# A two-layer graph kernel: five piece buffers in place of four, a shorter ring of rounded tiles, and the features loaded in six parts

## The chip, the cores and the metric

One core of one Trainium2 chip runs the kernel. The metric is the device time of one execution in microseconds. The engines are named as in the profile: PE (TensorE matmul), PEld (its weight loads), DVE (VectorE), ACT (ScalarE), POOL (GpSimd), SP (SyncE), and a trailing q (ACTq, SPq) is that engine's instruction queue, which issues DMAs.

## The reference

`x` is 4096 nodes by 128 features and `adj` a 4096 by 4096 float32 matrix (64 MiB) that is needed three times.

```python
h = relu(layernorm(x))
x = x + (adj.T @ h) / adj.sum(axis=0)[:, None]   # 0 where the sum is 0
h = relu(layernorm(x))
x1 = swish((adj @ h) @ W + b)
x2 = swish((adj @ x1) @ W + b)
return x + x2
```

## The kernel before

The kernel reads `adj` in three sweeps. No scheduler is involved: the program of each engine is written out by hand, and the order in the code is the order on the engine.

**Float32 products.** PE multiplies a float32 tile either whole (L367, L444) or split in two parts. For a split tile ACT writes the rounded part (`a_hi` at L542, `at_hi` in `hi3`, L584), POOL or DVE writes the rest (`a_lo` at L855, `at_lo` in `lo3`, L203), and PE then makes three cheap products: two with the rounded tile (main, L372 and L373, or L450 and L451) and one with the rest (L387, L461). A whole tile costs PE more time and the other engines nothing.

**Sweep 1** (`adj.T @ h`) takes 64 pairs of row tiles, v = 0 to 63, 16 to each quarter of the columns; a pair is 1 MiB and is loaded by SP (`load1`, L328) into one of `RAW1` = 5 buffers. `WHOLE1_FIRST`, `WHOLE1` and `WHOLE1_LAST` say which pairs of a quarter go whole. In the first quarter 6, 8, 9, 11, 12 and 14 are split. For each of them POOL first makes the rest of the features, `h_lo` (L846), and then the two rests of the pair, `a_lo` (L855). PE's main products of a split pair wait for `h_lo` (`h_lo_ready`, L360). Features of pairs that are split only later (`LATE_ROWS`) are rounded at the end of the quarter. DVE adds each pair to the degree sums (L699). The features `x_rows` themselves arrive in parts, `HEAD`, each loaded ahead of the pair in `HEAD_PAIRS`; for each part DVE makes statistics (L680, L683), POOL scale and shift (L833 to L838), and ACT the normed rows `h` (L509).

**Sweeps 2 and 3** (`adj @ h`, `adj @ x1`) are 8 groups of 512 nodes each, of four **pieces** of 2 MiB (512 rows by 1024 columns), in the order of `PIECES`. A piece is loaded in four blocks of 512 KB, 32 partitions each: SP issues blocks 0 and 1, ACT blocks 2 and 3 (`load3`, L285). There are `RAW3` = 4 piece buffers (`raw3`). A piece has four **units**; DVE turns a unit (`turn3`, L744) into one of `TURN` = 9 places of `turned`, or, for a few units, into PSUM (`dg`); its rest goes to the same place number of `at_lo`. ACT's rounded tiles lie in a ring of `RING3` = 6 places; ACT waits there until PE's main products and the rest of the unit six splits earlier are done (L581 to L583). PE makes main3 of a unit and then rest3 of the unit two before (`REST_LAG`). In a group of 16 units, 0, 5, 10 and 15 are whole; in even groups DVE makes the rests of units 3 and 13, in odd ones of 3, 8 and 13, and POOL all others.

After a pair of groups: ACT copies the sums out (`copy_n`, L592), PE multiplies by W (`xw`, L474), DVE adds the bias, ACT makes the swish (L600) and, in sweep 2, the rounded features of sweep 3 (L608), whose rest POOL makes (L869). Sweep 3 begins with the group that sweep 2 ended with, and the last four pieces of sweep 2 (`KEPT`) are used from their buffers and not loaded again.

**ACT's loop** (L638 to L659) does for each unit: `hi3(unit)`; in every fourth unit both blocks of the piece three ahead (L644, L645); then copies and swish when due. The two DMA issues stand in the same queue as the roundings, so a rounding behind them waits until they are issued.

```python
for unit in range(UNITS3):
    if not whole3(unit) and unit not in AHEAD3:
        hi3(unit)
    i = unit // QU + RAW3 - 1
    if unit == 1:
        load3(act, 3, ACT_BLOCKS)
    if unit % QU == 0 and RAW3 <= i < len(PIECES) and i not in KEPT:
        load3(act, i, ACT_BLOCKS)
```

Of the kernel before, what the change touches and what calls it, by code (L numbers as in the profile page):

```python
# [59 lines left out]
def build(nc, x_in, adj, w_in, b_in, out):  # L60
# [10 lines left out]
    with ctx:  # L71
# [40 lines left out]
        raw3 = {3: sb("raw3_3", [P, GB, BC], into=sweep2)}  # L112
        nT = sb("nT", [P, QC], into=sweep2)
        zs = sb("zs", [P, QT, P], into=sweep2)
        w = sb("w", [P, P], into=sweep2)
        bias = sb("bias", [P, P], into=sweep2)
        at_hi = sb("at_hi", [P, RING3, UC, GROUP], f32r, into=sweep2)
        for n in (1, 2):
            raw3[n] = sb(f"raw3_{n}", [P, GB, BC], into=sweep2)
        spare = sb("spare", [P, 256], into=sweep2)  # L120
# [79 lines left out]
        def lo3(eng, unit):  # L200
            s = split3(unit)
            eng.wait_ge(hi3_done, s + 1)
            return eng.tensor_tensor(at_lo[:, place(unit)], turned_tile(unit), at_hi[:, ring3(s)].bitcast(f32),  # L203
                                     ALU.subtract)
# [27 lines left out]
        def group_after(unit, later, hurried):  # L232

            ends = [n for n in range(2 * GROUPS) if last_unit(n) == unit - (hurried if n == GROUPS - 1 else later)]
            return ends[0] if ends else None
# [26 lines left out]
        def raw3_free(eng, i):  # L262
# [43 lines left out]

        def turned_nodes(dst, half=None):
# [10 lines left out]
        def _(sp):  # L318
# [30 lines left out]
        def _(pe):  # L349
# [76 lines left out]
            def main3(unit):  # L426
# [27 lines left out]
            def rest3(unit):  # L454
# [52 lines left out]
        def _(act):  # L507
# [63 lines left out]
            def hi3(unit):  # L571
# [12 lines left out]
                act.activation(at_hi[:, ring3(s)], turned_tile(unit), ACT.Copy).then_inc(hi3_done, 1)  # L584

            def copy_n(n):
                r = pair_of(n)
                act.wait_ge(main3_done, last_unit(n) + 1)
                act.wait_ge(rest3_done, split3(last_unit(n) - 1) + 1)
# [48 lines left out]
            for unit in range(UNITS3):  # L638
# [30 lines left out]
        def _(dve):  # L669
# [151 lines left out]
        def _(pool):  # L821
# [51 lines left out]
            for b, (lo, hi) in enumerate(HEAD):  # L873
                scale_shift(lo, hi, b)
            for v in splits1:
# [6 lines left out]
                lo1(v)  # L882
                if q >= 1 and k == 14:
# [38 lines left out]
```

## Time and profile before

| what | value |
|---|---|
| median of three runs (lowest, highest) | 626.46 us (625.41, 627.19) |
| the profiled execution's own time | 627.91 us |
| its span on the core | 626.1 us |
| PE busy | 609.1 us, 97% |
| POOL busy, DVE busy, ACT busy | 544.2, 541.8, 345.8 us |
| moved by DMA | 197.73 MB, mean 316 GB/s |
| granted TensorE clock | 0.998 of full speed |

Sweep 1 fills the span up to about 223 us, sweep 2 up to 423, sweep 3 the rest. A busy PE in this table is the union of overlapping records; where two records of PE follow each other without a gap it has no time to give.

### The profile page before, as it was taken

How to read it: one execution, taken by the hardware profiler on the slowest of the kernel's cores; microseconds unless marked ns; L12 is line 12 of the kernel's file. 1: busy time of each engine (PE TensorE's matmuls, PEld its weight loads, DVE VectorE, ACT ScalarE, POOL GpSimd, SP SyncE). 2: the span in 40 equal slices, each digit the busy share in tenths (PEclk: the TensorE clock that was granted, in tenths of full speed). 3: DMA queues.
4: the chain of work that ended last, by engine and by line, in shares of the span. 5: the costliest groups of instructions: out<-in, count | busy, mean ns of one | idle time of the engine just before them, and what ended most of it. 6: DMA issues, size and time to landing. Idle time of an engine off the chain costs nothing.

```text
span 626.1 us, 6939 instructions
## 1 busy us (share of the span) xinstructions
PE 609.1 (97%) x2296; PEld 413.3 (66%) x2296; DVE 541.8 (87%) x558; ACT 345.8 (55%) x456; POOL 544.2 (87%) x281
## 2 busy tenths in 40 slices
PE   8888999999999999999999999999999999999996
PEld 5355666577565567667667667777677677677774
DVE  5899699787868999897998998997998998998991
ACT  2493686595263354756656646646555546456551
POOL 2499799599688588999999989997999999998991
PEclk9999999999999999999999999999999999999999
DMA  9998999889999899999999999909999999999961
GB/s 324 382 372 301 339 320 358 293 329 275 353 351 367 287 345 334 347 347 347 347 347 348 347 348 347 283 25 220 308 348 349 348 349 348 348 348 349 348 176 34
DMA packets 151492, 197.73 MB, mean 316 GB/s; under 512 B 5280, under 2 KB 134560, under 8 KB 151456
## 3 DMA queue, kind: packets, MB, share of 16 engines
q1 hardware_dynamic: 86176, 132.92, 63.9%
q10 hardware_dynamic: 65280, 64.36, 33.6%
q8 instruction: 18, 0.29, 0.2%
q14 instruction: 18, 0.15, 0.1%
HBM read 195.17 MB, written 2.10 MB: 315 GB/s over the span
## 4 chain that ended last, share of the span: by engine, by line
PE 63%; POOL 10%; DMA 9%; issue 6%; DVE 6%; ACT 3%; ACTq 2%; SPq 1%; POOLq 0%; DVEq 0%
PE dg L444 14%; PE dg L461 11%; PE dg L451 11%; PE dg L450 11%; DMA raw<-in_adj_dram 9%; PE m_ps L367 7%; POOL a_lo L855 5%; POOL at_lo L203 3%; PE m_ps L372 2%; PE m_ps L387 2%; PE m_ps L373 2%; DVE dg L699 2%; PE m_ps L474 2%; ACTq L285 2%; DVE turned L744 2%
## 5 line engine op out<-in xcount | busy, mean ns | idle before, releaser
L203 POOL TENSOR_TENSOR at_lo<-turned,at_hi 128x1024 fp32r<-128x1024 f32 x152 | 358.9, 2402 | 26.5 <-ACT at_hi L584 26.4
L744 DVE STREAM_TRANSPOSE turned<-raw 128x1024 f32<-128x1024 f32 x216 | 257.7, 1221 | 20.2 <-PE dg L461 13.9
L584 ACT ACTIVATE at_hi<-turned 128x1024 fp32r<-128x1024 f32 x152 | 157.0, 1055 | 97.8 <-DVE turned L744 71.1
L855 POOL TENSOR_TENSOR a_lo<-raw,a_hi 128x1024 fp32r<-128x1024 f32 x62 | 145.9, 2391 | 21.7 <-ACT a_hi L542 21.6
L699 DVE TENSOR_TENSOR dg<-raw,dg 128x2048 f32<-128x2048 f32 x60 | 137.5, 2291 | 29.2 <-DMA raw<-in_adj_dram 27.6
L450 PE MATMUL dg<-at_hi,f_hi 128*128 128x512 f32 x384 | 152.4, 397 | 0.3 <-ACT at_hi L584 0.2
L451 PE MATMUL dg<-at_hi,f_lo 128*128 128x512 f32 x384 | 151.3, 394 | 0.0
L461 PE MATMUL dg<-at_lo,f_hi 128*128 128x512 f32 x384 | 145.1, 459 | 1.2 <-POOL at_lo L203 1.2
L444 PE MATMUL dg<-turned,f_w 128*128 128x512 f32 x256 | 120.2, 592 | 0.0
L367 PE MATMUL m_ps<-raw,h 128*128 128x512 f32 x264 | 117.8, 593 | 2.5 <-DMA raw<-in_adj_dram 1.7
L461 PEld LDWEIGHTS dg<-at_lo,f_hi 128*128 128x128 f32 x384 | 72.1, 188 | 43.3 <-issue 28.9
L367 PEld LDWEIGHTS m_ps<-raw,h 128*128 128x128 f32 x264 | 49.7, 189 | 55.5 <-issue 49.9
L542 ACT ACTIVATE a_hi<-raw 128x1024 fp32r<-128x1024 f32 x62 | 62.4, 1051 | 42.9 <-DMA raw<-in_adj_dram 41.9
L450 PEld LDWEIGHTS dg<-at_hi,f_hi 128*128 128x128 f32 x384 | 72.2, 188 | 17.9 <-ACT at_hi L584 1.4
L451 PEld LDWEIGHTS dg<-at_hi,f_lo 128*128 128x128 f32 x384 | 72.1, 188 | 16.8 <-issue 0.5
L444 PEld LDWEIGHTS dg<-turned,f_w 128*128 128x128 f32 x256 | 48.4, 189 | 36.5 <-issue 31.2
L372 PE MATMUL m_ps<-a_hi,h_hi 128*128 128x512 f32 x124 | 51.1, 412 | 5.4 <-issue 3.8
L203 DVE TENSOR_TENSOR at_lo<-dg,at_hi 128x1024 fp32r<-128x1024 f32 x40 | 47.6, 1189 | 3.9 <-ACT at_hi L584 3.9
L744 DVE STREAM_TRANSPOSE dg<-raw 128x1024 f32<-128x1024 f32 x40 | 49.3, 1233 | 1.7 <-PE dg L461 0.8
L373 PE MATMUL m_ps<-a_hi,h_lo 128*128 128x512 f32 x124 | 48.4, 391 | 0.0
L584 ACT ACTIVATE at_hi<-dg 128x1024 fp32r<-128x1024 f32 x40 | 40.8, 1020 | 13.3 <-DVE turned L744 9.3
L387 PE MATMUL m_ps<-a_lo,h_hi 128*128 128x512 f32 x124 | 42.4, 459 | 0.0
(55 smaller groups left out, 338.1 us busy)
## 6 DMA issues: line engine op xcount, KB each, us to landing
raw<-in_adj_dram SPq DMA_DIRECT2D x64, 1024.0 KB, 7.3
raw<-in_adj_dram ACTq DMA_DIRECT2D x122, 512.0 KB, 14.2
raw<-in_adj_dram SPq DMA_DIRECT2D x118, 512.0 KB, 12.5
out_dram<-x SPq DMA_DIRECT2D x12, 128.0 KB, 6.6
x_rows<-in_x_dram SPq DMA_DIRECT2D x2, 256.0 KB, 5.4
x_rows<-in_x_dram SPq DMA_DIRECT2D x1, 512.0 KB, 11.2
out_dram<-x SPq DMA_DIRECT2D x4, 64.0 KB, 1.8
out_dram<-x ACTq DMA_DIRECT2D x4, 64.0 KB, 2.0
```

The costliest lines, as they stand in the source:

```text
L203: return eng.tensor_tensor(at_lo[:, place(unit)], turned_tile(unit), at_hi[:, ring3(s)].bitcast(f32), ALU.subtract)
L367: mm = pe.matmul(acc, h[:, 2 * k + i], raw1[:, v % RAW1, i, cols], start=first, stop=last)
L372: pe.matmul(acc, h_hi[:, r], a_hi[:, s % RING1, cols], start=first, stop=False)
L444: mm = pe.matmul(acc, f_w[:, UC * WHOLE3.index(j) + c], turned[:, place(unit), c], start=first and c == 0, stop=False)
L450: pe.matmul(acc, f_hi[:, r + c], at_hi[:, s, c], start=first and c == 0, stop=False)
L451: mm = pe.matmul(acc, f_lo[:, r + c], at_hi[:, s, c], start=False, stop=False)
L461: mm = pe.matmul(dg[:, 0, (n % 2) * 512:(n % 2 + 1) * 512], f_hi[:, r + c], at_lo[:, place(unit), c], start=False, stop=unit + 1 == last_u ...
L542: act.activation(a_hi[:, s % RING1], raw1[:, v % RAW1, i], ACT.Copy).then_inc(hi1_done, 1)
L584: act.activation(at_hi[:, ring3(s)], turned_tile(unit), ACT.Copy).then_inc(hi3_done, 1)
L699: dve.tensor_tensor(dg[:, :, :], src, dg[:, :, :], ALU.add).then_inc(deg_added, 1)
L744: dve.transpose(dst, src).then_inc(t3_done, 1)
L855: pool.tensor_tensor(a_lo[:, s % RING1], raw1[:, v % RAW1, i], a_hi[:, s % RING1].bitcast(f32), ALU.subtract).then_inc(lo1_done, 1)
```

## The change

Six edits, made together.

1. The features come in six parts, ahead of pairs 0, 0, 1, 3, 5 and 7, where there were four, ahead of pairs 0, 2, 3 and 4. POOL's scale and shift of the sixth part stand behind its first split pair.
2. Pair 8 of the first quarter goes whole there, and is among the late rows.
3. A fifth piece buffer. It may be filled once sweep 1 is done on PE and DVE. Five pieces are kept between the sweeps.
4. The room comes from `turned` and `at_lo` (nine places become eight) and from the ring of rounded tiles (six become three).
5. ACT's two block issues of a piece stand two units apart.
6. The last two groups of sweep 2, and the first two of sweep 3, alternate piece by piece, so that each piece kept is again the one needed.

```diff
-HEAD = ((0, 4), (4, 8), (8, 16), (16, 32))
-HEAD_PAIRS = (0, 2, 3, 4)
+HEAD = ((0, 2), (2, 4), (4, 8), (8, 16), (16, 24), (24, 32))
+HEAD_PAIRS = (0, 0, 1, 3, 5, 7)
-WHOLE1_FIRST = (0, 1, 2, 3, 4, 5, 7, 10, 13, 15)
-LATE_ROWS = (2, 3, 5)
-SPLIT_ROWS = (6, 8, 9, 11, 12, 14) + LATE_ROWS
+WHOLE1_FIRST = (0, 1, 2, 3, 4, 5, 7, 8, 10, 13, 15)
+LATE_ROWS = (2, 3, 5, 8)
+SPLIT_ROWS = (6, 9, 11, 12, 14) + LATE_ROWS
-RAW3 = 4
-TURN = 9
-TURN_OFF = 4
+RAW3 = 5
+TURN = 8
+TURN_OFF = 3
-RING3 = 6
-RING_OFF = 2
+RING3 = 3
-PIECES = FIRST + tuple((n, q) for n in range(2, 2 * GROUPS) for q in range(QUARTERS))
+TAIL2 = ((6, 3), (7, 3), (6, 2), (7, 0), (6, 0), (7, 1), (6, 1), (7, 2))
+HEAD3 = tuple((n, q) for q in range(QUARTERS) for n in (GROUPS, GROUPS + 1))
+PIECES = (FIRST + tuple((n, q) for n in range(2, GROUPS - 2) for q in range(QUARTERS)) + TAIL2 + HEAD3
+          + tuple((n, q) for n in range(GROUPS + 2, 2 * GROUPS) for q in range(QUARTERS)))
...
         def raw3_free(eng, i):
...
+            elif i == 4:
+
+                eng.wait_ge(main1_done, QUARTERS * PAIRS)
+                eng.wait_ge(deg_added, QUARTERS * PAIRS)
...
             def hi3(unit):
...
-                if s == RING3 - RING_OFF:
-                    act.wait_ge(main1_done, QUARTERS * PAIRS)
-                    act.wait_ge(deg_added, QUARTERS * PAIRS)
                 if s >= RING3:
                     act.wait_ge(main3_done, splits3[s - RING3] + 1)
                     wait_lo3(act, splits3[s - RING3])
-                act.activation(at_hi[:, ring3(s)], turned_tile(unit), ACT.Copy).then_inc(hi3_done, 1)
+                act.activation(at_hi[:, s % RING3], turned_tile(unit), ACT.Copy).then_inc(hi3_done, 1)
...
-                if unit == 1:
-                    load3(act, 3, ACT_BLOCKS)
-                if unit % QU == 0 and RAW3 <= i < len(PIECES) and i not in KEPT:
-                    load3(act, i, ACT_BLOCKS)
+                if unit in (1, 2, 3, 5):
+                    load3(act, 3 + unit // 3, ACT_BLOCKS[(1, 2, 3, 5).index(unit) % 2:][:1])
+
+                if unit % QU in (0, 2) and RAW3 <= i < len(PIECES) and i not in KEPT:
+                    load3(act, i, ACT_BLOCKS[unit % QU // 2:unit % QU // 2 + 1])
...
-            for b, (lo, hi) in enumerate(HEAD):
+            for b, (lo, hi) in enumerate(HEAD[:-1]):
                 scale_shift(lo, hi, b)
...
                 lo1(v)
+                if v == splits1[0]:
+                    scale_shift(*HEAD[-1], len(HEAD) - 1)
```

**POOL in the first quarter.** `norm` are the columns of scale and shift, `h_lo` the rest of a pair's features, `a_lo` the rests of the pair. POOL before, from its fourth scale and shift on (line numbers of the kernel before):

```order
L833 TENSOR_TENSOR norm<-mv,consts 128x16
L834 TENSOR_TENSOR norm<-mv,consts 128x16
L836 TENSOR_TENSOR norm<-norm,consts 128x16
L838 TENSOR_TENSOR norm<-norm 128x16
L846 TENSOR_TENSOR h_lo<-h,h_hi 128x256
L855 TENSOR_TENSOR a_lo<-raw,a_hi 128x1024 x2
L846 TENSOR_TENSOR h_lo<-h,h_hi 128x256
L855 TENSOR_TENSOR a_lo<-raw,a_hi 128x1024 x2
```

POOL with the change, from the first split pair on (line numbers of the changed kernel):

```order
L860 TENSOR_TENSOR h_lo<-h,h_hi 128x256
L869 TENSOR_TENSOR a_lo<-raw,a_hi 128x1024 x2
L847 TENSOR_TENSOR norm<-mv,consts 128x8
L848 TENSOR_TENSOR norm<-mv,consts 128x8
L850 TENSOR_TENSOR norm<-norm,consts 128x8
L852 TENSOR_TENSOR norm<-norm 128x8
L860 TENSOR_TENSOR h_lo<-h,h_hi 128x256
L869 TENSOR_TENSOR a_lo<-raw,a_hi 128x1024 x2
```

The last part of the norm now stands between the first split pair (6) and the second, which is pair 9 and was pair 8; five split pairs are left of six.

**ACT where sweep 2 begins.** `raw_0` to `raw_4` are the piece buffers, `msgT` the last copy of sweep 1. ACT before, from that copy on; the rows of `raw_0` are piece 4, those of `raw_1` piece 5:

```order
L550 ACTIVATE msgT<-m_ps 128x2x8x32
L285 DMA raw_3<-in_adj_dram 32x16x256 x2
L584 ACTIVATE at_hi<-dg 128x1024
L584 ACTIVATE at_hi<-turned 128x1024
L285 DMA raw_0<-in_adj_dram 32x16x256 x2
L584 ACTIVATE at_hi<-turned 128x1024 x2
L647 DMA w<-in_L_gnn_W_dram 128x128
L648 DMA bias<-in_L_gnn_b_dram 128x128
L584 ACTIVATE at_hi<-turned 128x1024
L285 DMA raw_1<-in_adj_dram 32x16x256 x2
```

ACT with the change, from the same copy on; `raw_4` is piece 4, `raw_0` piece 5:

```order
L565 ACTIVATE msgT<-m_ps 128x2x8x32
L297 DMA raw_3<-in_adj_dram 32x16x256 x2
L596 ACTIVATE at_hi<-dg 128x1024
L297 DMA raw_4<-in_adj_dram 32x16x256
L596 ACTIVATE at_hi<-turned 128x1024
L297 DMA raw_0<-in_adj_dram 32x16x256
L297 DMA raw_4<-in_adj_dram 32x16x256
L596 ACTIVATE at_hi<-turned 128x1024
L297 DMA raw_0<-in_adj_dram 32x16x256
L596 ACTIVATE at_hi<-turned 128x1024
L660 DMA w<-in_L_gnn_W_dram 128x128
L661 DMA bias<-in_L_gnn_b_dram 128x128
```

The rounding from `dg` is unit 3, the next one unit 4, the two after it (one row before, two rows now) units 6 and 7. From unit 3 on, ACT had issued two blocks ahead of unit 6 and none between 6 and 7; it now issues three ahead of unit 6 and a fourth between 6 and 7.

## Rows read from the trace of the kernel before

**Rows 1.** The page: busy time by engine, and the costliest group of instructions

```profile
PE 609.1 (97%) x2296; PEld 413.3 (66%) x2296; DVE 541.8 (87%) x558; ACT 345.8 (55%) x456; POOL 544.2 (87%) x281
...
L203 POOL TENSOR_TENSOR at_lo<-turned,at_hi 128x1024 fp32r<-128x1024 f32 x152 | 358.9, 2402 | 26.5 <-ACT at_hi L584 26.4
```

**Rows 2.** Windows: a pair of groups of sweep 2, and one of sweep 3

```profile
core 0: us, PE busy (x) PEld busy (x) DVE busy (x) ACT busy (x) POOL busy (x), PEclk, DMA share, GB/s
301.36:350.48 49.12, 49.12 (x194) 34.94 (x192) 45.59 (x40) 29.27 (x33) 47.83 (x23) 1.00 1.10 348
...
472.14:520.59 48.45, 48.45 (x193) 34.88 (x192) 45.25 (x39) 26.17 (x27) 45.47 (x20) 1.00 1.10 348
```

**Rows 3.** Timeline of PE (start, us, what, idle before), first 52 us

```profile
7.76 13.97 PE L367 MATMUL m_ps<-raw,h 128*128 128x512 f32 x32 [0.77 <-ACT h L509]
23.43 7.13 PE L367 MATMUL m_ps<-raw,h 128*128 128x512 f32 x16 [1.69 <-DMA raw<-in_adj_dram]
...
40.94 0.47 PE L372 MATMUL m_ps<-a_hi,h_hi 128*128 128x512 f32 x1 [2.13 <-issue]
...
51.70 0.47 PE L372 MATMUL m_ps<-a_hi,h_hi 128*128 128x512 f32 x1 [1.63 <-issue]
```

**Rows 4.** Chain that ended last (start, us, what), pair 13, and the start of quarter two

```profile
54.67 3.43 PE m_ps L367 x8
...
65.19 6.87 PE m_ps L367 x16
```

**Rows 5.** Timeline of POOL and ACT in the first quarter

```profile
34.72 0.73 POOL L846 TENSOR_TENSOR h_lo<-h,h_hi 128x256 fp32r<-128x256 f32 x1
35.41 4.74 POOL L855 TENSOR_TENSOR a_lo<-raw,a_hi 128x1024 fp32r<-128x1024 f32 x2
...
50.87 0.73 POOL L846 TENSOR_TENSOR h_lo<-h,h_hi 128x256 fp32r<-128x256 f32 x1
...
37.01 2.01 ACT L542 ACTIVATE a_hi<-raw 128x1024 fp32r<-128x1024 f32 x2 [0.21 <-DMA raw<-in_adj_dram]
```

**Rows 6.** Timeline of ACT and its queue where sweep 2 begins

```profile
213.51 2.33 ACTq L285 DMA_DIRECT2D raw<-in_adj_dram  x4
...
223.79 0.86 ACTq L285 DMA_DIRECT2D raw<-in_adj_dram  x2
...
225.09 3.12 ACTq L285 DMA_DIRECT2D raw<-in_adj_dram  x2
...
228.33 1.06 ACT L584 ACTIVATE at_hi<-turned 128x1024 fp32r<-128x1024 f32 x1 [1.66 <-issue]
...
252.68 0.32 ACTq L285 DMA_DIRECT2D raw<-in_adj_dram  x1
...
270.43 2.90 ACTq L285 DMA_DIRECT2D raw<-in_adj_dram  x1
```

**Rows 7.** Timeline of POOL, same stretch

```profile
227.70 9.47 POOL L203 TENSOR_TENSOR at_lo<-turned,at_hi 128x1024 fp32r<-128x1024 f32 x4
...
243.68 4.76 POOL L203 TENSOR_TENSOR at_lo<-turned,at_hi 128x1024 fp32r<-128x1024 f32 x2 [1.57 <-ACT at_hi L584]
...
248.83 1.63 POOL L836 TENSOR_TENSOR norm<-norm,consts 128x8 f32<-128x8 f32 x1
...
261.93 11.79 POOL L203 TENSOR_TENSOR at_lo<-turned,at_hi 128x1024 fp32r<-128x1024 f32 x5
```

**Rows 8.** Timeline of PE: waits of sweep 2 and 3, then units 1 and 4 of group 13

```profile
266.72 0.73 PE L461 MATMUL dg<-at_lo,f_hi 128*128 128x512 f32 x2 [0.69 <-POOL at_lo L203]
...
296.27 0.50 PE L450 MATMUL dg<-at_hi,f_hi 128*128 128x512 f32 x1 [0.25 <-ACT at_hi L584]
...
548.57 0.39 PE L451 MATMUL dg<-at_hi,f_lo 128*128 128x512 f32 x1
...
551.09 0.39 PE L450 MATMUL dg<-at_hi,f_hi 128*128 128x512 f32 x1
```

**Rows 9.** Chain that ended last: one block of a piece, from its issue

```profile
270.43 15.85 DMA raw<-in_adj_dram
```

More of the change, by code:

```diff
@@ L111, in build @@
         f3_w = sb("f3_w", [P, UC * len(WHOLE3), P], into=sweep2)
-        raw3 = {3: sb("raw3_3", [P, GB, BC], into=sweep2)}
+        raw3 = {n: sb(f"raw3_{n}", [P, GB, BC], into=sweep2) for n in (3, 4)}
+        zs = sb("zs", [P, QT, P], into=sweep2)
         nT = sb("nT", [P, QC], into=sweep2)
-        zs = sb("zs", [P, QT, P], into=sweep2)
         w = sb("w", [P, P], into=sweep2)
         bias = sb("bias", [P, P], into=sweep2)
+        spare = sb("spare", [P, 256], into=sweep2)
         at_hi = sb("at_hi", [P, RING3, UC, GROUP], f32r, into=sweep2)
@@ L119, in build @@
             raw3[n] = sb(f"raw3_{n}", [P, GB, BC], into=sweep2)
-        spare = sb("spare", [P, 256], into=sweep2)
         turned = sb("turned", [P, TURN, UC, GROUP], into=whole_tiles)
@@ L202, in lo3 @@
             eng.wait_ge(hi3_done, s + 1)
-            return eng.tensor_tensor(at_lo[:, place(unit)], turned_tile(unit), at_hi[:, ring3(s)].bitcast(f32),
+            return eng.tensor_tensor(at_lo[:, place(unit)], turned_tile(unit), at_hi[:, s % RING3].bitcast(f32),
                                      ALU.subtract)
@@ L224, in first_unit, with last_split, closing @@
             return min(QU * i for i in range(len(PIECES)) if PIECES[i][0] == n)
+        def last_split(n):
+            return max(unit for unit in splits3 if PIECES[unit // QU][0] == n)
+        def closing(n):
+            if last_split(n) + REST_LAG >= last_unit(n):
+                return last_split(n), True
+            return last_unit(n), False
         def piece_loads(i):
@@ L232, in group_after @@
         def group_after(unit, later, hurried):
-            ends = [n for n in range(2 * GROUPS) if last_unit(n) == unit - (hurried if n == GROUPS - 1 else later)]
+            ends = [n for n in range(2 * GROUPS) if last_unit(n) == unit - (hurried if n in (GROUPS - 2, GROUPS - 1) else later)]
             return ends[0] if ends else None
@@ L305, in store, with head_parts @@
                    .then_inc(y_out, 16)
+        def head_parts(v):
+            return [b for b in range(len(HEAD)) if HEAD_PAIRS[b] == v]
         def turned_nodes(dst, half=None):
@@ L331, in _ @@
             for v in range(QUARTERS * PAIRS):
-                if v in HEAD_PAIRS:
-                    b = HEAD_PAIRS.index(v)
+                for b in head_parts(v):
                     lo, hi = HEAD[b]
@@ L444, in main3 @@
                         mm = pe.matmul(acc, f_w[:, UC * WHOLE3.index(j) + c], turned[:, place(unit), c],
-                                       start=first and c == 0, stop=False)
+                                       start=first and c == 0, stop=closing(n) == (unit, False) and c == UC - 1)
                 else:
-                    s, r = ring3(split3(unit)), UC * SPLIT3.index(j)
+                    s, r = split3(unit) % RING3, UC * SPLIT3.index(j)
                     pe.wait_ge(hi3_done, split3(unit) + 1)
@@ L461, in rest3 @@
                     mm = pe.matmul(dg[:, 0, (n % 2) * 512:(n % 2 + 1) * 512], f_hi[:, r + c], at_lo[:, place(unit), c],
-                                   start=False, stop=unit + 1 == last_unit(n) and c == UC - 1)
+                                   start=False, stop=closing(n) == (unit, True) and c == UC - 1)
                 mm.then_inc(rest3_done, 1)
@@ L588, in copy_n @@
                 act.wait_ge(main3_done, last_unit(n) + 1)
[L589 removed]
+                act.wait_ge(rest3_done, split3(last_split(n)) + 1)
                 act.wait_ge(xw_done, r) if r >= 1 else None
@@ L764, in residual @@
                    .then_inc(y_ready, 1)
-            head(0)
+            for b in head_parts(0):
+                head(b)
             for v in range(QUARTERS * PAIRS):
                 add_degrees(v)
-                if v < len(HEAD) - 1:
-                    head(v + 1)
+                for b in head_parts(v + 1):
+                    head(b)
                 q, k = v // PAIRS - 1, v % PAIRS
```

2 lines of the change are left out of this document (removed).

## Prediction

> **What bounds the kernel now.** I read the page first. PE is busy for 97% of the span, POOL and DVE for 87% each [rows 1]. The windows say more. In sweeps 2 and 3 two groups take 49.12 us and 48.45 us, PE is busy for every microsecond of them, and the DMA queues are full as well (348 GB/s) [rows 2]. So in two thirds of the kernel PE has no gap to give back. Nothing that only moves loads, buffers or ACT's work can shorten it there; it can only open a gap. POOL stands close behind: 47.83 us of 49.12 in a pair of groups of sweep 2, 45.47 of 48.45 in sweep 3 [rows 2], at 2.40 us for each rest [rows 1].
>
> What can be won lies where PE waits, and the timeline of PE shows where. In the first quarter it waits 1.69 us for the matrix ahead of pair 4, 2.13 us ahead of pair 9 and 1.63 us ahead of pair 12, and it starts 0.77 us after the last rest because the first normed rows are late [rows 3]. The two waits called "issue" end when POOL has made `h_lo` of the pair: the second ends at 51.70, and POOL's `h_lo` of pair 12 runs from 50.87 to 51.60 [rows 3, 5]. In the first quarter PE is thus paced by POOL, 0.73 + 4.74 = 5.4 us for each split pair (34.72 to 40.15) [rows 5]. Later waits are small: 0.69 us for POOL at 266.72, 0.25 us for ACT at 296.27 [rows 8].
>
> **The change, part by part.** The sum is made against the profiled execution, 627.91 us, which is 1.45 above the median of the three runs, 626.46; the difference is then taken from the median.
>
> *The first quarter (features in six parts, pair 8 whole).* These belong together, because one chain decides: when `h_lo` of pair 12 is ready. After it PE runs without a wait to the end of the quarter, from 51.70 to 65.19, 13.5 us [rows 3, 4]. POOL's list loses pair 8 (5.4 us) but may not start pair 9 before its data: ACT rounds the first half of pair 9 from 37.01, when it lands, to 38.0 [rows 5]. The bytes ahead of pair 9 are the same, so it lands no sooner. The sixth part's scale and shift, whose longest step takes 1.63 us for eight columns [rows 7], fall in the pause before 37, when POOL, free of pair 8, has nothing else. From there: two rests of pair 9, `h_lo` of 11, two rests of 11, `h_lo` of 12: 38.0 + 4.74 + 0.73 + 4.74 + 0.73 = 48.9, where it was 51.6. Is PE there by then? Its work grows by 0.5 to 0.7 us: pair 8 whole takes 3.43, as the one at 54.67, where a split one, as from 51.70 to 54.67, takes 2.97 with the start of a wait in it [rows 3, 4]. It wins more than that ahead of pair 9, where 1.69, 2.13 and 0.77 us of waits stand [rows 3], even if a wait of about 1 us for pair 7 comes, whose data lands no sooner. So the quarter ends 51.6 - 48.9 = **2.7 us earlier**. Bounds: nothing, if the small parts delay the first pairs as much as they help; and 6.2 - 0.5 = 5.7 us, if all four waits of [rows 3] went and nothing came. I take 2.7, which one chain of rows gives. From 65.19 on PE takes pair after pair without a gap [rows 4], so the gain is handed on to sweep 2.
>
> *ACT's issues at the start of sweep 2.* Here the change costs. An issue takes 0.32 us when the queue has room, and 2.90 us when it is full [rows 6]. How full is read from one block: issued at 270.43, the issue over at 273.33, landed at 286.28 [rows 6, 9]. So the queue lets ACT go 12.95 us ahead of the landing. At half of 348 GB/s a block of 0.524 MB takes 3.0 us, so ACT can have 4.3 blocks under way and each further one must wait for 3.0 us of draining. Before, ACT issues four blocks at 213.51, two at 223.79, and the seventh and eighth from 225.09 to 228.21; the rounding of unit 6 stands behind them and starts at 228.33, after 1.66 us called "issue" [rows 6]. With five buffers a ninth block stands ahead of unit 6 and a tenth ahead of unit 7. They can be issued at 228.2 + 3.0 = 231.2 and 234.2. Unit 6 is then rounded at 232.3, where POOL would have begun it at 227.70 + 2.37 = 230.07 [rows 7], and unit 7 at 235.3. The thirteenth block, ahead of unit 13, follows at 228.2 + 15.0 and some 1.4 us for W and bias, 244.6; unit 13 is rounded at 245.7, and POOL takes it up 2.0 us later than at 243.68 [rows 7]. From there to the rest that PE waits for at 266.72 POOL has no pause over 0.1 us [rows 7, 8], so PE is **2.0 us later**. Bounds: nothing, if an issue is never held; 4.3 us, if POOL's first pause (232.3 - 230.07 = 2.2) and that of unit 7's round come on top of each other.
> A rule speaks the other way. The Trainium skill, page "DMA: Bandwidth & Descriptors", section "Issuing engines are not separate DMA queues", says that issuing on several engines saves only sequencer time, "usually small relative to the DMA itself"; by it this term would be 0 and the sum -2.4. The 2.90 us row speaks against it.
>
> *The swish of the first pair of groups.* It stands behind an issue too, and the rounding behind it already comes 0.25 us late [rows 8]. One more held issue costs between 0 and 0.9 us; I take 0.3.
>
> *Ring of three, eight places.* ACT may round a unit once PE's main products of three splits before are done. The tightest place in a group is unit 4, since unit 5 is whole and units 1 to 4 follow each other: unit 1's last record ends at 548.57 + 0.39 = 548.96, unit 4's first is at 551.09 [rows 8]. That leaves 2.13 us for a rounding of 1.05 us [rows 6]: 1.1 us to spare. At units 9 and 14 a whole tile lies between, and more is left. POOL's rests: behind unit 4's rounding it has nine or ten of 2.40 us until the next unit 4, 21.6 to 24.0 us in a group of 24.2 to 24.6 (half of [rows 2]), and the pair's W product makes the fuller group the longer. So it fits: **0**, covered by 1.1 us. Bound above: case C. Eight places let DVE turn a unit when PE is one unit further; PE follows by several units, so 0 too.
>
> *Fifth buffer, five kept, alternate groups.* 2 MiB less are loaded, 6 us of a full queue, but sweep 3 has no wait for data that it could end: 0.
>
> Sum: -2.7 + 2.0 + 0.3 = -0.4, so 627.5 for such an execution and **626.1** against the median. About 0.3%, 1.9 us, is what a measurement of this kernel can tell from no change.
>
> **The rivals.**
>
> *B, issues cost nothing.* Issues two units apart are 3 us apart, which is just the draining time of a block, so each may find room at 0.32 us. Then the first quarter's 2.7 us stand, and up to 1 us of POOL's pause of 1.57 us, which ends with an ACT rounding [rows 7], goes too: 626.46 - 3.2 = 623.3. For it: the edit sets them apart. Against: with one more piece under way the queue is fuller than before, and it is full now.
>
> *C, slower: the ring of three.* ACT now may not be held for over 1.1 us before unit 4. If an issue of 2.90 us falls there, or a copy or swish with it, PE waits 2.9 + 1.05 - 2.13, up to 1.8 us, before the rests come late to POOL, which has 1 to 3 us in a pair to make it up [rows 2]. It decides from a hold of 1.1 us. At 0.4 us in each of some 13 groups it is +5.2: 626.1 + 5.2 = 631.3. For it: before, ACT could be six splits ahead and used it. Against: unit 2's issue, the one just before, waits for a queue that PE's own pace keeps 3 us ahead.
>
> *D, the buffers' places.* The same work takes 49.12 us in sweep 2 and 48.45 in sweep 3 [rows 2], 0.67 in a pair, 2.7 over four. The trace doesn't say why. If it hangs on where tiles lie, which the change moves, it can go (623.4) or come in sweep 3 as well (628.8). The Trainium skill, page "SBUF — State Buffer", section "SBUF: two separate sides", says that PE never waits on anyone there; by it the case doesn't exist.
>
> **How the numbers follow.** Forecast (within 624.6 to 628.3): 0.42. B: 0.26. C: 0.22. D: 0.10, half to each side. The likeliest is 626.1. The range takes in B, D and the forecast with its bounds, and C up to just below its price: 622.3 to 631.0. Faster by over 0.3%: 0.26 + 0.05 and 0.02 from the forecast's lower edge, 0.33. Slower: 0.22 + 0.05 = 0.27. Within: 0.40.
>
> **What would show it.** Right: PE's wait ahead of pair 12 ends near 49, quarter two begins near 62.5; ACT's issues around unit 6 take 2 to 3 us; POOL pauses before unit 6's rest and PE is again where it was by 267 to 297; pairs of groups stay at 49.1 and 48.5. Wrong: issues of 0.3 us all through sweep 2 (B); PE waiting for ACT once in each group (C); pairs of 48.4 in sweep 2 or 49.1 in sweep 3 (D); or a first quarter that ends after 64.

## The result and the profile after

The changed kernel takes **632.57 us** (median of 5 runs, 629.6 to 633.05), the kernel before 626.46 beside it; the ratio on record is 1.0088, interval 1.0072 to 1.0105. (The ratios here and below are those on record; they can differ by about 0.001 from the quotient of the two medians.) It is 6.1 us slower than the kernel before. The forecast was 626.1, and 632.57 lies above its range, 622.3 to 631.0. Repeated later beside other kernels, it took 630.72 us beside 626.37, ratio 1.0064 (1.0040 to 1.0087): slower again, though this median would lie just inside the range. The profiled execution of after is the shortest of its five, 629.6 us with a span of 627.8.

The page of after, busy time and the group of POOL's rests (compare [rows 1]; the last column is POOL's idle time ahead of them, 34.3 us where it was 26.5):

```profile
PE 612.1 (97%) x2292; PEld 413.0 (66%) x2292; DVE 539.8 (86%) x558; ACT 345.7 (55%) x453; POOL 542.0 (86%) x287
...
L206 POOL TENSOR_TENSOR at_lo<-turned,at_hi 128x1024 fp32r<-128x1024 f32 x152 | 359.4, 2404 | 34.3 <-ACT at_hi L596 34.2
```

PE in the first quarter of after, from its timeline (compare [rows 3]). The wait ahead of pair 4 and that of pair 9 are gone, smaller ones for the matrix have come (0.62 us ahead of pair 7), and the one ahead of pair 12 ends at 49.44 in place of 51.70:

```profile
7.63 21.04 PE L382 MATMUL m_ps<-raw,h 128*128 128x512 f32 x48 [0.92 <-DMA raw<-in_adj_dram]
...
32.15 3.70 PE L382 MATMUL m_ps<-raw,h 128*128 128x512 f32 x8 [0.62 <-DMA raw<-in_adj_dram]
...
49.44 0.47 PE L387 MATMUL m_ps<-a_hi,h_hi 128*128 128x512 f32 x1 [1.20 <-issue]
```

Where the time went is read from windows that begin and end with the same units. The first 32 units of sweep 2 and the first 32 of sweep 3, before:

```profile
223.53:275.38 51.85, 50.63 (x199) 34.90 (x198) 48.86 (x67) 28.66 (x36) 49.05 (x26) 1.00 1.10 343
423.30:472.14 48.84, 48.74 (x194) 34.80 (x193) 43.89 (x38) 28.65 (x32) 44.97 (x23) 1.00 1.07 296
```

The same two of after, and between and behind them a pair of groups of each sweep (compare [rows 2]):

```profile
220.27:275.22 54.95, 52.19 (x200) 36.14 (x198) 48.88 (x66) 28.95 (x36) 49.24 (x25) 0.97 1.10 343
324.74:373.88 49.14, 49.14 (x193) 34.95 (x192) 43.91 (x39) 28.52 (x32) 47.02 (x24) 1.00 1.10 348
423.02:473.84 50.82, 49.70 (x193) 34.33 (x192) 44.28 (x39) 28.32 (x32) 47.86 (x23) 1.00 1.10 286
473.84:522.30 48.46, 48.46 (x194) 34.88 (x192) 44.67 (x39) 26.77 (x28) 45.39 (x20) 1.00 1.10 337
```

So sweep 2 begins 3.3 us earlier (220.27 for 223.53), its start takes 3.1 us more, the start of sweep 3 2.0 us more, and the pairs between are as they were. That is the whole difference of the two profiled spans, 627.8 - 626.1. Only a part of it shows as idle PE, 2.76 us for 1.22 in the first window and 1.12 for 0.10 in the second. The rest counts as busy: pauses that a record of PE covers (such as 450.65 to 451.02, where records otherwise follow 0.23 us apart) and, in the first window, a slower clock (last section).

The start of sweep 2, ACT and its queue in after (compare [rows 6]):

```profile
225.44 2.84 ACTq L297 DMA_DIRECT2D raw<-in_adj_dram  x1
228.40 1.06 ACT L596 ACTIVATE at_hi<-turned 128x1024 fp32r<-128x1024 f32 x1 [4.17 <-DVE turned L757]
228.42 2.79 ACTq L297 DMA_DIRECT2D raw<-in_adj_dram  x1
231.33 1.06 ACT L596 ACTIVATE at_hi<-turned 128x1024 fp32r<-128x1024 f32 x1 [1.88 <-PE dg L459]
231.35 2.79 ACTq L660 DMA_DIRECT2D w<-in_L_gnn_W_dram  x1
234.16 0.69 ACTq L661 DMA_DIRECT2D bias<-in_L_gnn_b_dram  x1
234.98 1.06 ACT L596 ACTIVATE at_hi<-turned 128x1024 fp32r<-128x1024 f32 x1 [2.58 <-POOL at_lo L206]
```

Each of these roundings, of units 6, 7 and 8, starts 0.12 to 0.13 us after the issue ahead of it has ended, whatever engine the view puts the wait down to. One issue of 2.8 us stands ahead of each; the third is that of W, 64 KB, which takes as long as that of a block, with 0.69 us for the bias behind it. PE then has nothing left to do until unit 8 is rounded:

```profile
236.18 0.47 PE L465 MATMUL dg<-at_hi,f_hi 128*128 128x512 f32 x1 [2.09 <-ACT at_hi L596]
...
237.94 0.63 PE L465 MATMUL dg<-at_hi,f_hi 128*128 128x512 f32 x1
```

The start of sweep 3 was not foreseen as a place at all. POOL has two pauses there (ACT, for its part, waits 3.77 us for PE ahead of 433.55), then it runs without any, and ACT and PE wait for it. POOL, ACT and PE of after:

```profile
428.00 4.71 POOL L206 TENSOR_TENSOR at_lo<-turned,at_hi 128x1024 fp32r<-128x1024 f32 x2 [0.99 <-ACT at_hi L596]
434.68 2.42 POOL L206 TENSOR_TENSOR at_lo<-turned,at_hi 128x1024 fp32r<-128x1024 f32 x1 [1.97 <-ACT at_hi L596]
437.05 2.13 POOL L883 TENSOR_TENSOR f_lo<-zs,f_hi 128x256 fp32r<-128x256 f32 x3
439.14 23.56 POOL L206 TENSOR_TENSOR at_lo<-turned,at_hi 128x1024 fp32r<-128x1024 f32 x10
...
433.55 1.06 ACT L596 ACTIVATE at_hi<-turned 128x1024 fp32r<-128x1024 f32 x1 [3.77 <-PE dg L466]
...
444.01 1.06 ACT L596 ACTIVATE at_hi<-turned 128x1024 fp32r<-128x1024 f32 x1 [1.29 <-POOL at_lo L206]
...
455.69 0.74 PE L476 MATMUL dg<-at_lo,f_hi 128*128 128x512 f32 x2 [0.68 <-POOL at_lo L206]
```

### The profile page after: what moved, and what is told of

It reads as the page before. It is cut to its first block, busy times and chain, and to the rows that moved or that the text cites. A ratio compares the mean times of both kernels' runs of the same rounds, so it can differ in the third digit from the quotient of the medians.

```text
span 627.8 us, 6936 instructions
## 1 busy us (share of the span) xinstructions
PE 612.1 (97%) x2292; PEld 413.0 (66%) x2292; DVE 539.8 (86%) x558; ACT 345.7 (55%) x453; POOL 542.0 (86%) x287
## 4 chain that ended last, share of the span: by engine, by line
PE 68%; POOL 11%; issue 6%; DMA 5%; DVE 5%; ACT 3%; SPq 1%; ACTq 0%; POOLq 0%; DVEq 0%
PE dg L459 16%; PE dg L476 13%; PE dg L465 12%; PE dg L466 12%; PE m_ps L382 7%; DMA raw<-in_adj_dram 5%; POOL a_lo L869 5%; POOL at_lo L206 5%; PE m_ps L489 2%; PE m_ps L402 2%; PE m_ps L387 2%; PE m_ps L388 2%; DVE dg L712 2%; DVE turned L757 1%; SPq L344 1%
## 5 line engine op out<-in xcount | busy, mean ns | idle before, releaser
L206 POOL TENSOR_TENSOR at_lo<-turned,at_hi 128x1024 fp32r<-128x1024 f32 x152 | 359.4, 2404 | 34.3 <-ACT at_hi L596 34.2
L596 ACT ACTIVATE at_hi<-turned 128x1024 fp32r<-128x1024 f32 x152 | 158.8, 1058 | 152.0 <-PE dg L466 100.5
L869 POOL TENSOR_TENSOR a_lo<-raw,a_hi 128x1024 fp32r<-128x1024 f32 x60 | 141.4, 2393 | 21.7 <-ACT a_hi L557 21.3
L382 PE MATMUL m_ps<-raw,h 128*128 128x512 f32 x272 | 121.6, 593 | 1.5 <-DMA raw<-in_adj_dram 1.5
L382 PEld LDWEIGHTS m_ps<-raw,h 128*128 128x128 f32 x272 | 51.0, 189 | 56.7 <-issue 51.0
L557 ACT ACTIVATE a_hi<-raw 128x1024 fp32r<-128x1024 f32 x60 | 60.2, 1050 | 40.9 <-DMA raw<-in_adj_dram 40.3
L387 PE MATMUL m_ps<-a_hi,h_hi 128*128 128x512 f32 x120 | 49.3, 411 | 2.2 <-issue 1.2
L388 PE MATMUL m_ps<-a_hi,h_lo 128*128 128x512 f32 x120 | 46.8, 390 | 0.0
```

Source lines behind the costliest of these rows:

```text
L382: mm = pe.matmul(acc, h[:, 2 * k + i], raw1[:, v % RAW1, i, cols], start=first, stop=last)
L387: pe.matmul(acc, h_hi[:, r], a_hi[:, s % RING1, cols], start=first, stop=False)
L557: act.activation(a_hi[:, s % RING1], raw1[:, v % RAW1, i], ACT.Copy).then_inc(hi1_done, 1)
L596: act.activation(at_hi[:, s % RING3], turned_tile(unit), ACT.Copy).then_inc(hi3_done, 1)
L869: pool.tensor_tensor(a_lo[:, s % RING1], raw1[:, v % RAW1, i], a_hi[:, s % RING1].bitcast(f32), ALU.subtract).then_inc(lo1_done, 1)
```

## The experiments

Three causes were set against each other: **Q**, one more piece under way keeps ScalarE's queue full and ScalarE behind its issues; **R**, the ring of three; **O**, the alternating groups. Each kernel ran beside the kernel before on the same chip. The changed kernel itself was repeated in only one of the three sets, so its 630.72 us and the times of most kernels built on it come from different chips: differences between them are read with the ratios to the kernel before, and from the windows. The first window below is always the first 32 units of sweep 2, the second those of sweep 3.

**The first-quarter edits alone** (on the kernel before: HEAD, HEAD_PAIRS, WHOLE1_FIRST, LATE_ROWS, SPLIT_ROWS, the head parts, the sixth scale and shift).

> The kernel before with the first-quarter edits alone (features in six parts, pair 8 whole, the sixth part's scale and shift after the first rests); four buffers, ring of six and order of pieces stay. Theory (the first quarter's gain is real and only the later edits lose it): PE's cumulative waits fall by 3 us by 65 us and stay so; 626.5 - 3.0 = 623.5 us, ratio 0.995. Rival (the gain would have been lost at the start of sweep 2 anyway, since the loads or ACT's copies there set the time): 625.5 to 626.5, ratio 0.999 to 1.000.

625.48 us, ratio 0.9991 (0.9973 to 1.0009): the time that the rival named, and no measurable gain. The place is another than the rival's, though: the first quarter's gain is there in the trace, and most of it is gone before sweep 2 begins. To see where, the kernel before was profiled a second time:

> The kernel before, for a second profile: its runs spread from 624.5 to 629.2 us, its profiled one was 627.9. If a faster one is met, the stretch in which PE waits less than in the first profile shows what varies; I expect 1 to 2 us less between 160 and 220 us.

This time its profiled execution (a single one, on another chip than that of the first-quarter edits) took 624.99 us, 2.9 less than the first. Windows 180 to 210 us, of the kernel before in its first profile, of the same in its second, and of the first-quarter edits alone (three kernels' answers, one fence each):

```profile
180.00:210.00 30.00, 28.34 (x98) 17.54 (x97) 23.21 (x37) 10.85 (x12) 28.01 (x13) 1.00 0.99 333
```

```profile
180.00:210.00 30.00, 29.85 (x105) 18.93 (x104) 26.03 (x38) 10.04 (x10) 29.18 (x16) 1.00 1.02 363
```

```profile
180.00:210.00 30.00, 29.41 (x99) 17.60 (x98) 25.96 (x38) 9.84 (x10) 28.23 (x16) 1.00 0.99 349
```

PE is idle for 1.66, 0.15 and 0.59 us of them. The idle time shows only a part of what is lost; two rows of the same work in each kernel (PE transposes the sums) show the whole, second profile of before, then the first-quarter edits:

```profile
177.80 0.64 PE L423 MATMUL tp<-ident,msgT 128*128 128x128 f32 x4
...
196.09 0.60 PE L423 MATMUL tp<-ident,msgT 128*128 128x128 f32 x4
```

```profile
175.87 0.64 PE L426 MATMUL tp<-ident,msgT 128*128 128x128 f32 x4
...
195.74 0.60 PE L426 MATMUL tp<-ident,msgT 128*128 128x128 f32 x4
```

With the edits PE is 1.9 us ahead at the first and 0.35 at the second. The reason is in ACT's timeline, second profile of before, then the first-quarter edits:

```profile
192.33 2.01 ACT L542 ACTIVATE a_hi<-raw 128x1024 fp32r<-128x1024 f32 x2 [5.92 <-DMA raw<-in_adj_dram]
195.41 2.01 ACT L542 ACTIVATE a_hi<-raw 128x1024 fp32r<-128x1024 f32 x2 [1.07 <-DMA raw<-in_adj_dram]
```

```profile
192.21 2.01 ACT L545 ACTIVATE a_hi<-raw 128x1024 fp32r<-128x1024 f32 x2 [6.33 <-DMA raw<-in_adj_dram]
195.09 2.01 ACT L545 ACTIVATE a_hi<-raw 128x1024 fp32r<-128x1024 f32 x2 [0.87 <-DMA raw<-in_adj_dram]
```

The matrix comes at nearly the same moment, 192.2 to 192.3 and 195.1 to 195.4, whether PE is ahead or not, and ACT rounds it as it lands. So of PE's 1.9 us 0.3 are left at the start of sweep 2, 220.36 for 220.70. In the first profile of before the loads there were later still: ACT waits for the matrix until 195.46 and 198.26, the same two rows of PE stand at 178.14 and 199.04, and sweep 2 began at 223.53. How long this place takes varies from profile to profile: sweep 2 begins at 220.70, 222.12 (the ring of three alone) and 223.53 without the first-quarter edits, and with them between 220.22 and 222.37 in ten profiles and at 225.02 in an eleventh (ScalarE's issues together). What makes it vary stays open.

**The ring of three alone** (on the kernel before).

```diff
-RING3 = 6
-RING_OFF = 2
+RING3 = 3
+RING_OFF = 0
+        room3 = sb("room3", [P, 2, UC, GROUP], into=sweep2)
         at_hi = sb("at_hi", [P, RING3, UC, GROUP], f32r, into=sweep2)
+        room4 = sb("room4", [P, 1, UC, GROUP], into=sweep2)
```

(With `RING_OFF` at 0 ACT's wait for the end of sweep 1 also stands ahead of the fourth split in place of the fifth.)

> The kernel before with at_hi of three places in place of six (the room of the other three stays empty, so that every other tile keeps its place); nothing else. Theory R (the ring of three makes ACT, POOL and PE wait for each other): slower, by 2 to 5 us, 628.5 to 631.5, with ACT's roundings waiting for POOL's rests and PE waiting for ACT in places; POOL idle at sweep 2's start for longer. Rival Q (the fuller queue of the fifth buffer is what costs) and rival O (the alternating groups put POOL's heavy units together): no change, 626.0 to 627.0.

626.97 us, ratio 1.0007 (0.9990 to 1.0025): no change that can be told. Not R by itself: the start of sweep 2 takes what it took before, 51.86 us, that of sweep 3 0.4 us more:

```profile
222.12:273.98 51.86, 51.11 (x200) 34.79 (x198) 48.72 (x68) 29.06 (x36) 49.08 (x25) 1.00 1.10 343
421.78:471.04 49.26, 49.02 (x193) 34.74 (x192) 43.46 (x38) 27.76 (x31) 46.42 (x23) 1.00 1.06 284
```

**The changed kernel again.**

> The changed kernel again, for its second profile and times beside the others of this set: 629.5 to 633 us. If its longer runs are a stall of their own (three of five were 3 us over the profiled one), the profile may show one of them: then some stretch has waits of PE of 3 us that the first profile lacks.

630.72 us; the profiled one took 629.61 and shows the same stalls at the same places. The longer runs were not caught.

**ScalarE's issues of a piece together** (on the changed kernel; the rest too).

```diff
-                if unit in (1, 2, 3, 5):
-                    load3(act, 3 + unit // 3, ACT_BLOCKS[(1, 2, 3, 5).index(unit) % 2:][:1])
-                if unit % QU in (0, 2) and RAW3 <= i < len(PIECES) and i not in KEPT:
-                    load3(act, i, ACT_BLOCKS[unit % QU // 2:unit % QU // 2 + 1])
+                if unit in (1, 3):
+                    load3(act, 3 + unit // 3, ACT_BLOCKS)
+                if unit % QU == 0 and RAW3 <= i < len(PIECES) and i not in KEPT:
+                    load3(act, i, ACT_BLOCKS)
```

> The changed kernel with ScalarE's two block issues of a piece together again (ahead of the piece's first unit, and those of pieces 3 and 4 after units 1 and 3), nothing else. If issues apart are what spares ACT: slower, by 1 to 4 us, with two issues of 2.9 us in a row and the ring of three run dry behind them. If an issue into a full queue takes its 2.8 us wherever it stands: the same within 1 us, 629 to 633.

633.56 us, ratio 1.0127 (1.0093 to 1.0161); the profiled execution was the longest of its six, 637.84 us, with a late start of sweep 2, so only its window is compared. The two blocks' issues take 3.8 and 5.7 us ahead of a rounding, and the first 32 units take 57.99 us in place of 54.95. So issues apart do spare ScalarE something: the longer it stands behind them, the longer the start takes.

```profile
226.27 3.80 ACTq L297 DMA_DIRECT2D raw<-in_adj_dram  x2
...
230.22 5.72 ACTq L297 DMA_DIRECT2D raw<-in_adj_dram  x2
236.06 1.06 ACT L596 ACTIVATE at_hi<-turned 128x1024 fp32r<-128x1024 f32 x1 [4.81 <-PE dg L459]
```

**All blocks from piece 3 on by SyncE** (on the changed kernel: SyncE's `load3` takes SP_BLOCKS + ACT_BLOCKS, ScalarE's four lines above go).

> The changed kernel with all four blocks of every piece from piece 3 on issued by SyncE (ScalarE keeps those of pieces 0 to 2, W, the bias and the stores at the end). Theory Q (ScalarE's issues into a full queue cost the start of sweep 2 its 3 us): PE's cumulative waits between 200 and 300 us are 3.7 us, as in the kernel with the first-quarter edits alone, where they are 6.7; 3 us faster than the changed kernel, 627 to 628 us. The stall at 440 to 460 us stays. Rival: SyncE's queue alone doesn't carry 348 GB/s, or the blocks of a piece in one queue come later; then PE waits for data and the kernel is as slow or slower, over 631 us.

811.91 us, ratio 1.29: the rival, and far beyond it. Slices of the page in sweep 2 move 214 to 217 GB/s where two queues moved 348. Nearly all blocks in one queue don't feed this kernel, so the run says nothing on Q.

**The plain order of pieces, none kept** (on the changed kernel).

```diff
-PIECES = (FIRST + tuple((n, q) for n in range(2, GROUPS - 2) for q in range(QUARTERS)) + TAIL2 + HEAD3
-          + tuple((n, q) for n in range(GROUPS + 2, 2 * GROUPS) for q in range(QUARTERS)))
+PIECES = FIRST + tuple((n, q) for n in range(2, 2 * GROUPS) for q in range(QUARTERS))
-KEPT = range(SWEEP2, SWEEP2 + RAW3)
+KEPT = ()
-            return i // RAW3 + (1 if i < SWEEP2 else 0)
+            return i // RAW3 + 1
```

> The changed kernel with the plain order of pieces (a group's four pieces one after the other, in all but the first two groups) and, since five buffers then don't match, no piece kept: five pieces more are loaded, 10.5 MB or 30 us of a full queue. Theory O (the alternating groups put POOL's rests and lo_x1 close together and make the stall): PE loses under 0.9 us between 420 and 460 us, where it loses 2.2; 629 us, unless the five loads cost anything. Theory R (ring of three): the stall of 2 us stays, 631 us.

628.56 us, ratio 1.0029 (1.0018 to 1.0041), 2.2 us faster than the changed kernel (by the medians; the intervals just touch) although it loads 10.5 MB more. The start of sweep 3 takes 49.27 us in place of 50.82; what is left over 48.84 is as much as the ring of three alone cost, 0.4. The start of sweep 2, 55.70, is no faster than the changed kernel's 54.95:

```profile
220.22:275.92 55.70, 51.80 (x200) 36.33 (x199) 48.86 (x66) 29.23 (x36) 49.91 (x25) 0.97 1.10 343
423.33:472.60 49.27, 49.02 (x193) 34.72 (x192) 44.15 (x38) 28.11 (x31) 46.85 (x23) 1.00 1.10 338
```

**A ring of four, seven unit places** (on the changed kernel: TURN 8 to 7, TURN_OFF 3 to 2, RING3 3 to 4).

> The changed kernel with at_hi of four places and seven unit places (the memory of one goes to the other). Theory R: with one more split ahead ACT rides over part of its holds; the start loses 1 us less and the stall at 440 to 460 us 1 us less, 629 us. Theories Q and O: within 0.7 us of the changed kernel, 630 to 631.5; the stall there keeps over 1.7 us.

629.65 us, ratio 1.0040 (1.0025 to 1.0056), which by itself can't be told from the changed kernel's 1.0064. The windows tell more: the start of sweep 3 takes 49.09 us, and POOL runs from 414.86 to 471.25 there without the two pauses; the start of sweep 2 takes 55.65. So the stall of sweep 3 needs both, the order and the ring of three; undoing either takes most of it away. The start of sweep 2 is helped by neither, against what R expected of it.

**ScalarE's blocks one piece later** (on the changed kernel). Five buffers stay, with SyncE's half of each piece as early as ever.

```diff
-                i = unit // QU + RAW3 - 1
-                if unit in (1, 2, 3, 5):
-                    load3(act, 3 + unit // 3, ACT_BLOCKS[(1, 2, 3, 5).index(unit) % 2:][:1])
-                if unit % QU in (0, 2) and RAW3 <= i < len(PIECES) and i not in KEPT:
+                i = unit // QU + RAW3 - 2
+                if unit in (1, 2):
+                    load3(act, 3, ACT_BLOCKS[unit - 1:unit])
+                if unit % QU in (0, 2) and 4 <= i < len(PIECES) and i not in KEPT:
```

> The changed kernel with ScalarE's two blocks of each piece issued one piece (four units) later, so that its half of the queue is as deep as with four buffers, while SyncE's half uses all five. Theory Q (ScalarE stands behind its issues because one piece more is under way; that is the 3.0 us which PE loses more between 220 and 300 us): PE loses 3.7 us between 200 and 300 us, as with four buffers, where the changed kernel loses 6.7; 627.5 to 628.5 us. The stall at 440 to 460 us stays. Rival: the loss at the start comes from the ring of three or from the order of the first units, and stays at 6.7: 630 to 631.5 us.

625.59 us, ratio 0.9975 (0.9959 to 0.9990): 5.1 us faster than the changed kernel, more than expected, and the two intervals lie apart. Up to unit 16 ScalarE's issues take 0.3 to 0.6 us and the W issue 1.0, and the first 32 units take 50.66 us, less even than before; the stall of sweep 3 stays (50.84), with the ring of three and the order as they were. This is Q, shown for the start of sweep 2. Part of what it gives is more than going back: ScalarE's blocks are now as late as in the kernel before, but one at a time, where that kernel issued both together (225.09, 3.12 us).

Its ACT queue, and its two windows:

```profile
226.68 0.32 ACTq L297 DMA_DIRECT2D raw<-in_adj_dram  x1
227.55 1.01 ACTq L659 DMA_DIRECT2D w<-in_L_gnn_W_dram  x1
...
229.43 0.61 ACTq L297 DMA_DIRECT2D raw<-in_adj_dram  x1
```

```profile
220.59:271.25 50.66, 50.23 (x200) 35.13 (x199) 47.24 (x65) 29.35 (x36) 49.30 (x26) 1.00 1.10 343
418.66:469.50 50.84, 49.72 (x194) 34.33 (x193) 44.27 (x39) 28.34 (x32) 47.89 (x23) 1.00 1.03 267
```

**VectorE for one rest more in each of the first two groups of sweep 3** (on the changed kernel; in `by_dve`, `+ ((7,) if n in (GROUPS, GROUPS + 1) else ())`).

> The changed kernel with VectorE in place of POOL for the rest of the eighth unit of the first two groups of sweep 3 (four rests by VectorE among their first sixteen units, where two are; 4.8 us less for POOL). Theory O (POOL's share of these units is over what PE's pace leaves, and with a ring of three nothing carries it): the stall at 440 to 460 us falls from 2.2 us to under 0.8; 628.5 to 629.5 us. If the stall comes from late data at the start of sweep 3, or from ACT, it stays at 2 us: 630.5 us.

628.19 us, ratio 1.0028 (1.0009 to 1.0047), 2.5 us faster than the changed kernel by the medians, with intervals that overlap. The windows decide: the start of sweep 3 takes 48.51 us, without a gap of PE, although POOL's two pauses are still there (1.01 and 1.98 us), and sweep 2's start stays at 54.93. O is shown for sweep 3: it is POOL's share there that is too large.

```profile
221.15:276.08 54.93, 50.74 (x199) 34.92 (x198) 48.76 (x66) 28.79 (x36) 49.17 (x26) 1.00 1.10 343
423.92:472.43 48.51, 48.51 (x193) 34.88 (x192) 45.96 (x41) 28.21 (x32) 43.80 (x21) 1.00 1.10 290
```

**The kernel before with the first-quarter edits, W and bias issued by SyncE** ahead of its piece 5 (behind the waits for the last pair, since their room is raw1's before).

> The kernel before with the first-quarter edits, and W and bias issued by SyncE ahead of piece 5 in place of by ScalarE at unit 7 (there they hold ScalarE for 2.7 us in a full queue). Theory Q: ScalarE rounds units 8 to 12 up to 2.7 us earlier, POOL is ahead by as much, and of the 3.7 us that PE loses between 240 and 300 us 1.5 to 2.5 go: 623 to 624 us, ratio 0.996. Rival (ScalarE is then held as long by the next block): no change from the kernel with the first-quarter edits alone, 625 to 625.5 us.

**623.22 us**, ratio 0.9937 (0.9918 to 0.9956): faster than both kernels. Sweep 2's first 32 units take 50.36 us where the first-quarter edits alone take 52.06. With the issue of W gone from ScalarE the rounding of unit 8 starts at 229.07, 7.67 us into sweep 2, where it started 8.90 us into it (229.26) with the first-quarter edits alone, behind 2.07 us for W and 0.68 for the bias:

```profile
226.56 2.01 ACT L593 ACTIVATE at_hi<-turned 128x1024 fp32r<-128x1024 f32 x2 [2.02 <-issue]
229.07 1.06 ACT L593 ACTIVATE at_hi<-turned 128x1024 fp32r<-128x1024 f32 x1 [0.49 <-DVE turned L749]
```

**The changed kernel mended**: ScalarE's blocks late, VectorE's two rests, W and bias by SyncE, as above.

> The changed kernel with all three of this set: ScalarE's blocks one piece later, VectorE for the two rests more, W and bias by SyncE. If the two causes (ScalarE's issues at the start, POOL's share at the start of sweep 3) are the whole of the loss, it gets back 3.0 and 2.0 us and 1 to 2 of the W issue: 624 to 625.5 us. If something else is in it (for one, whatever makes its runs up to 3 us longer than the profiled one), it stays above 627 us.

**623.39 us**, ratio 0.9940 (0.9918 to 0.9962), slightly better than expected: 7.3 us under the changed kernel. The two starts take 50.67 and 48.52 us; that W is issued by SyncE added nothing here to the 50.66 of the late blocks alone. It takes the same time as the kernel with four buffers and a ring of six above, measured beside it, which has the same first quarter and the same issue of W. So the causes found are the whole of the loss, and the later edits together (fifth buffer, five kept pieces, smaller rings), even with their two losses mended, bring nothing that can be measured; the fifth buffer was not tried alone.

## Why the prediction was wrong

Two steps failed: the handing on of the first quarter's gain, and the 0 for the alternating order. A third term, ACT's issues, was right in mechanism and too small.

*The first quarter, -2.7.* Right where it was looked at: `h_lo` of pair 12 is ready at 49.3 (forecast 48.9), PE's wait for it ends at 49.44, and sweep 2 began 3.3 us earlier than in the first profile. The step that failed is "From 65.19 on PE takes pair after pair without a gap [rows 4], so the gain is handed on to sweep 2". PE has no gap up to 180, but at 186 to 200 us the matrix comes late, and a PE that is earlier waits for it. Against the second profile of before the gain is 0.3 to 0.4 us; alone it gave 0.9 in the medians, which the interval can't tell from nothing. The profile read was one of a slow pass through this place. That it lay 1.45 us over the median was known and set aside as an offset; it was time lost in one place, with 1.66 us of idle PE where the second profile has 0.15. That the 3.3 us against the first profile are near 2.7 is luck: a part of them is that slow pass.

*ACT's issues, +2.0.* Right in mechanism, in place and nearly in times: units 6 and 7 were rounded at 228.40 and 231.33 where 232.3 and 235.3 were forecast, on the clock of a sweep 2 that began 3.3 us later. The size was wrong, 3.1 us (51.85 to 54.95), or 3.0 against the second profile:

```profile
220.70:272.65 51.95, 50.66 (x200) 34.92 (x199) 48.74 (x68) 28.62 (x36) 49.02 (x25) 1.00 1.10 343
```

The term's path went from the block ahead of unit 13 through POOL's list to the rest that PE waits for at 266.72. PE runs dry before that, for 2.09 us at 236.18. The issues of W and the bias stand ahead of unit 8 and take 2.79 and 0.69 us, where "some 1.4 us for W and bias" was taken (1.54 and 0.68 us in before, at 229.60), and with the two blocks ahead of them the delay reaches PE directly. The Trainium skill ("DMA: Bandwidth & Descriptors", section "Issuing engines are not separate DMA queues") calls the time that an issue takes "usually small relative to the DMA itself", and the prediction set beside its own term what follows if it is taken as nothing: 0 us. Here the trace disagrees with that reading: an issue took 2.8 us, which is a fifth of the 15.85 us from a block's issue to its landing [rows 9] but about the 3.0 us in which one block drains, and the issues together cost the kernel 3.1 us. With an emptier queue (0.32 us) the sentence holds.

*The swish of the first pair, +0.3.* PE waits for ACT at 296 for 0.12 us in after, below what the view marks (a record ends at 295.86, the next starts at 295.98), where it waited 0.25 in before. So nothing was added; within the bounds.

*Ring of three, 0; five kept and alternate groups, 0.* The first holds alone (+0.4 in one place, ratio 1.0007), the second fails with it: 2.0 us. "Sweep 3 has no wait for data that it could end" asked only what the order does for loads. It also moves POOL's rests. With two groups taken in turn, the 16 units from the ninth of sweep 3 on hold eleven rests of POOL's (nine of them in the first twelve, with none of VectorE's), and the rests of the x1 features (`f_lo`, 2.1 us) fall among them: 11 x 2.4 + 2.1 = 28.5 us, where PE takes half of 48.84, 24.4. In the plain order the same 16 units hold ten, and the first twelve seven: for those twelve 7 x 2.4 + 2.1 = 18.9 us against PE's 18.3, where the alternating order has 9 x 2.4 + 2.1 = 23.7. Such an excess is borne if POOL is ahead: with a ring of four, in the same order, it has no pause from 414.86 to 471.25, and the start takes 49.09 us. With three places ACT waits for PE and POOL for ACT (pauses of 0.99 and 1.97 us between 427 and 435), and POOL can't make up for it. Rival C asked for a place where the ring decides, but looked for one in each group and for an issue; it is one place, set by POOL.

*Rivals.* B fell: issues took 2.8 us. C as written fell (pairs stay 49.14 and 48.46); that its price, 631.3, is near the measured times is coincidence. D did not come: buffers and rings lie elsewhere, and a pair of each sweep takes what it took. Why a pair of sweep 2 takes 0.7 us more than one of sweep 3 stays open.

*The sum as it should have stood:* -0.4 + 3.0 + 2.0 = +4.6 against the second profile of before, whose span is 4.6 shorter than that of after. Added to the median this is 631.1; measured were 630.72 and 632.57. What makes a run of the changed kernel up to 3 us longer than the profiled ones stays open; the kernel with VectorE's two rests more shows it as well (eight of twelve runs at 627.4 to 629.0 us, four at 630.2 to 630.6).

## What to carry over

In this kernel an engine that both issues loads and feeds another stood still while its queue was full, for 2.8 us at a block of 512 KB and as long at the 64 KB of W. So count each of its issues, small ones too, at up to the draining time of a block (3.0 us here), and issue later rather than earlier once the queue is kept full. A gain early in a kernel is worth what the next place bound by data leaves of it, and whether there is one is seen only from the landing times with the work moved ahead; a second profile of the same kernel costs little and shows which waits come and go. When an order of pieces changes, add up each helper engine's work per stretch anew, not per sweep.

## What was not expected of the hardware

TensorE's granted clock is 1.00 in every window of before read here. In after it falls behind the wait of 2.09 us at 236.18, to 0.50, which is 1.2 GHz in place of 2.4, and is back at 1.00 at 242 to 244; its matmuls there come 0.43 us apart (237.94 above, 238.37) and not 0.23:

```profile
238.37 0.63 PE L466 MATMUL dg<-at_hi,f_lo 128*128 128x512 f32 x1
```

```profile
236.00:238.00 2.00, 1.82 (x7) 1.47 (x8) 1.83 (x9) 0.99 (x2) 1.89 (x1) 0.82 1.10 347
238.00:240.00 2.00, 2.00 (x6) 1.59 (x5) 1.25 (x1) 0.60 (x1) 2.00 (x2) 0.50 1.10 349
240.00:242.00 2.00, 2.00 (x7) 1.11 (x5) 1.26 (x1) 0.58 (x2) 2.00 (x2) 0.82 1.10 348
```

It did not make the 3.1 us: the kernel with VectorE's two rests more had the same wait (2.08 us at 237.01), kept 1.00 all through this stretch and took 54.93 us for it, against 54.95. A PE at half the clock only waited less later, 0.39 us at 255.18 where the other waited 1.84 at 256.04. So after the same wait of PE the clock fell in one kernel and not in the other. In the plain order and with the ring of four it stayed at 1.00 behind the first wait (2.10 and 2.09 us) and fell to 0.50 behind the second (1.80 and 1.87 us); these two took 55.70 and 55.65 us. That the lower clock cost them the 0.7 us is likely, not shown.

SyncE's queue alone moved 214 to 217 GB/s of these 0.5 MB blocks (32 partitions, runs of 1 KB), SyncE's and ScalarE's together 348. It isn't the queue alone that sets this: at 196 to 200 us the one queue of SyncE moved 409 GB/s with sweep 1's 1 MB loads, and at 184 to 192, where both kinds are under way, 305 to 339 were moved (the first-quarter edits alone).
